# A gated block with a mixture of experts: the last batch's shared network as four steps behind the experts, and integers transposed from the low halves of rounded floats

## What is computed

```python
def smooth_quant_linear(x, w):                    # [T, D] and [O, D] -> [T, O]
    s  = sqrt(max(amax_cols(|x|), EPS) / max(amax_cols(|w|), EPS))
    xs, ws = x / s, w * s
    x_scale = max(amax_rows(|xs|), EPS) / 127     # w_scale likewise
    x_q = clip(round(xs / x_scale), -127, 127)    # w_q likewise
    return x_q @ w_q.T * x_scale * w_scale.T

def layer(x, guw, dw):                            # one batch; guw 512x512, dw 512x256
    gate, up = split(smooth_quant_linear(x, guw))
    return smooth_quant_linear(silu(gate) * up, dw)

def moe(x):                                       # 2048 tokens; 16 experts, top 2, capacity 256
    w, e = top_k(softmax(x @ gate_w.T), 2)
    y  = the two experts' outputs of each token, times w
    sh = (silu(x @ ws_gate) * (x @ ws_up)) @ ws_down         # inner size 704
    return y + sh                                            # an expert's inner size is 352

x = x + tanh(g_xattn) * layer(layernorm(x), fside, ctx)      # per batch
x = x + tanh(g_ffn) * moe(layernorm(x))
```

## Time and profile before

| | before |
|---|---|
| median of three runs | 679.56 us (679.54 to 680.46) |
| the profiled execution | 680.59 us |
| its span, first to last instruction | 678.9 us |
| PE busy | 519.1 us, 76% of the span |
| DVE busy | 423.3 us, 62% |
| ACT busy | 291.3 us, 43% |
| POOL busy | 156.1 us, 23% |
| mean granted clock of TensorE | 0.909 |
| moved by DMA | 83.32 MB, mean 123 GB/s |

### The profile page before, as it was taken

How to read it: one execution, slowest core, us unless ns; L and a number is a source line. 1 busy time by engine, 2 the same in 40 slices (tenths; PEclk the granted TensorE clock), 3 DMA queues, 4 the chain that set the end, 5 groups by cost and what they waited for, 6 DMA issues and landing times.

```text
span 678.9 us, 8404 instructions
## 1 busy us (share of the span) xinstructions
PE 519.1 (76%) x3080; PEld 423.7 (62%) x3080; DVE 423.3 (62%) x633; ACT 291.3 (43%) x402; POOL 156.1 (23%) x138
## 2 busy tenths in 40 slices
PE   0363424799899989899789999999999999994000
PEld 0232322588557866587557889999999999994000
DVE  5667788596677757642658486666666666660354
ACT  2267553426632673243232145566556655651000
POOL 2311454022000400010000151231122113001773
PEclk9995765999899998999899989999999999998555
DMA  7810103001110001300100157776787677602776
GB/s 288 308 62 0 32 0 124 1 1 32 62 63 0 31 0 62 127 1 0 63 0 1 32 175 239 254 242 202 254 262 239 192 263 259 202 31 81 244 246 233
DMA packets 42200, 83.32 MB, mean 123 GB/s; under 512 B 4081, under 2 KB 22513, under 8 KB 41153
## 3 DMA queue, kind: packets, MB, share of 16 engines
q1 hardware_dynamic: 37056, 66.23, 28.4%
q0 software_dynamic: 5120, 16.78, 8.1%
HBM read 66.23 MB, written 16.78 MB: 122 GB/s over the span
## 4 chain that ended last, share of the span: by engine, by line
PE 64%; DVE 15%; ACT 8%; issue 6%; POOL 5%; DMA 1%; POOLq 0%; DVEq 0%
PE ps_gu L1098 12%; PE ps_gu L1100 12%; PE ps_gu L1099 12%; PE ps_d L1098 5%; PE ps_d L1100 5%; PE ps_d L1099 5%; POOL got L484 4%; PE ps_a L1137 2%; PE ps_a L1332 2%; DVE y L745 1%; PE ps_a L1144 1%; DVE bn_b L734 1%; DVE sh_hid L819 1%; PE ps_a L1198 1%; ACT w L517 1%
## 5 line engine op out<-in xcount | busy, mean ns | idle before, releaser
L1098 PE MATMUL ps_gu<-ex_xhi,w_hi 128*128 128x256 f32 (+1 forms) x384 | 110.3, 287 | 1.1 <-DVE ex_xlo L1038 1.1
L1099 PE MATMUL ps_gu<-ex_xlo,w_hi 128*128 128x256 f32 (+1 forms) x384 | 107.9, 281 | 0.0
L1100 PE MATMUL ps_gu<-ex_xhi,w_lo 128*128 128x256 f32 (+1 forms) x384 | 107.7, 281 | 0.0
L1098 PE MATMUL ps_gu<-xt_hi,sw_hi 128*128 128x512 f32 x176 | 72.0, 409 | 7.5 <-DVE sh_hid L819 7.2
L1098 PEld LDWEIGHTS ps_gu<-ex_xhi,w_hi 128*128 128x128 f32 (+1 forms) x384 | 69.6, 181 | 6.1 <-issue 3.9
L1099 PEld LDWEIGHTS ps_gu<-ex_xlo,w_hi 128*128 128x128 f32 (+1 forms) x384 | 69.5, 181 | 0.7
L1100 PEld LDWEIGHTS ps_gu<-ex_xhi,w_lo 128*128 128x128 f32 (+1 forms) x384 | 69.7, 181 | 0.0
L1099 PE MATMUL ps_gu<-xt_lo,sw_hi 128*128 128x512 f32 x176 | 68.9, 392 | 0.0
L1100 PE MATMUL ps_gu<-xt_hi,sw_lo 128*128 128x512 f32 x176 | 68.9, 391 | 0.0
L453 POOL DMA_INDIRECT xg<-x2n_scratch,idx_col x32 | 52.1, 1629 | 18.0 <-POOL idx_col L449 13.1
L1024 DVE TENSOR_TENSOR w_lo<-raw_gu,w_hi 128x1408 fp32r<-128x1408 f32 x32 | 51.6, 1616 | 0.0
(11 more groups left out here) (234 smaller groups left out, 1129.4 us busy)
## 6 DMA issues: line engine op xcount, KB each, us to landing
raw_gu<-in_L_ffn_w_gate SPq DMA_DIRECT2D x16, 704.0 KB
raw_gu<-in_L_ffn_w_up SPq DMA_DIRECT2D x16, 704.0 KB
raw_d<-in_L_ffn_w_down SPq DMA_DIRECT2D x16, 512.0 KB
expert_out_scratch<-eo SPq DMA_DIRECT2D x16, 512.0 KB
w<-in_fside_BxS2xS SPq DMA_DIRECT2D x4, 1024.0 KB, 5.2
x2n_scratch<-y SPq DMA_DIRECT2D x4, 1024.0 KB, 3.9
out<-x SPq DMA_DIRECT2D x8, 512.0 KB
x<-in_x SPq DMA_DIRECT2D x1, 3072.0 KB, 16.8
```

The lines of the kernel that those rows point to most:

```text
L1098: pe.matmul(dst, a_hi, b_hi, start=start, stop=False)
L1099: pe.matmul(dst, a_hi, b_lo, start=False, stop=False)
L1100: return pe.matmul(dst, a_lo, b_hi, start=False, stop=stop)
```

## The change

1. *Rounding.* `rounded` goes. `quantise` adds 16384 with the magic number, so the low 16 bits of each rounded float are 16384 plus the integer. PE transposes these low halves directly as bfloat16 (every second one), and `integers` reads the bank as 16-bit integers and takes 16384 off. The semaphores `x_scaled` and `w_scaled` go, and the loads of `w1` and `w2` wait for the transposes.
2. *Shared network.* The last iteration does only chunks 0 to 2 of batch 2's shared network, the routing's stage chunks 3 to 5 of it. Batch 3's shared network becomes four steps E to E+3 behind the experts, with an expert's sizes: 256 tokens (steps E, E+2 the first half, E+1, E+3 the second) by 352 of the inner size (E, E+1 the first, E+2, E+3 the second). The weights of a half are loaded and split once, its tokens too. DVE adds each step's result from `ps_d` to `x2` (`shared_rows`). Batch 3's transposed tokens for the router go to their own place (`xt3_hi`, `xt3_lo`).
3. *End.* `got` holds three batches. POOL's gathers start when all experts' rows are stored, beside the four steps, and `add_rows` is written out between and behind the steps' DVE work.

The diff, cut to its core:

```diff
+LOW16 = 16384.0
...
+    got = [place(cur, "got0", [P, J, 2, D]), place([region], "got1", [P, J, 2, D]), place([shared], "got2", [P, J, 2, D])]
+    FL, FM = B - 2, 3
+    NE, NW = E + 4, E + 2
...
-            sp.wait_ge(qw_done[LA], 1)
+            sp.wait_ge(full[LA], unit(LA, 0, A_QW + 1))
             load_w1(1)
...
-            sp.wait_ge(sh_gu, MS * B)
+            sp.wait_ge(sh_gu, MS * (FL + 1))
             load_raw(1, 1)
...
+            def load_tokens(e, q):
+                sp.wait_ge(ex_xt, e - 1)
+                j = slice((e - E) * HALF, (e - E + 1) * HALF)
+                sp.dma_start(xg[q][:], x2n_v[B - 1][:, j, :]).then_inc(xf_in[q], 16)
...
+            store_eo(E - 4, 0)
+            split_done(E - 2)
+            load_shared(E, 0)
+            load_tokens(E, 0)
+            store_eo(E - 3, 1)
+            split_done(E - 1)
+            load_shared(E + 1, 1)
+            load_tokens(E + 1, 1)
+            store_eo(E - 2, 0)
+            store_eo(E - 1, 1)
...
             gather_rows(0, 0)
+            pool.wait_ge(ex_wlo, 2 * E + 2)
+            pool.wait_ge(ex_wdlo, E + 1)
             gather_rows(1, 1)
-            with pool.Fori(1, B // 2) as r:
-                for k in range(2):
-                    pool.wait_ge(summed, 2 * (2 * r + k - 1))
-                    gather_rows(2 * r + k, k)
+            pool.wait_ge(ex_wlo, 2 * NW)
+            pool.wait_ge(ex_wdlo, NW)
+            pool.wait_ge(got_in[0][0], 16 * J)
+            pool.wait_ge(got_in[0][1], 16 * J)
+            gather_rows(2, 2)
+            pool.wait_ge(got_in[1][0], 16 * J)
+            pool.wait_ge(got_in[1][1], 16 * J)
+            pool.wait_ge(summed, 2)
+            gather_rows(3, 0)
...
                 for j in range(J):
-                    last = act.activation(src[:, j, :], src[:, j, :], ACT.Copy, bias=MAGIC, scale=inv[:, j:j + 1])
-                last.then_inc(scaled, 1)
-                rounded(b, src, dst, scaled, done)
+                    last = act.activation(src[:, j, :], src[:, j, :], ACT.Copy, bias=MAGIC + LOW16, scale=inv[:, j:j + 1])
+                last.then_inc(done, 1)
...
-                src = bank(layer, n0 + u, wide).bitcast(BF16)
+                src = bank(layer, n0 + u, wide).bitcast(I16)
                 act.activation(dst[:, 2 * u:2 * u + 2, :], src.rearrange("p (c t) -> p c t", c=2),
-                               ACT.Copy).then_inc(free[layer], 1)
+                               ACT.Copy, bias=-LOW16).then_inc(free[layer], 1)
...
-            iteration(None, B - 1, B - 2)
+            iteration(None, B - 1, FL, FM)
...
+            def shared_rows(e):
+                dve.wait_ge(ex_d, M * e + M)
+                if e >= E + 2:
+                    dve.wait_ge(ex_eo, e - 1)
+                for h in range(HALF):
+                    j = e % 2 * HALF + h
+                    last = dve.scalar_tensor_tensor(out=x2[:, B - 1, j, :], in0=ps_d[:, 2 * (e % 2) + h, :], scalar=tg[:, 1:2],
+                                                    in1=x2[:, B - 1, j, :], op0=ALU.mult, op1=ALU.add)
+                last.then_inc(ex_eo, 1)
...
+            hidden(E + 2, 0, 0)
+            shared_rows(E + 1)
+            hidden(E + 2, 0, 1)
+            add_rows(0, 0)
+            hidden(E + 2, 0, 2)
+            add_rows(0, 1)
+            hidden(E + 3, 1, 0)
+            shared_rows(E + 2)
+            hidden(E + 3, 1, 1)
+            add_rows(1, 0)
+            hidden(E + 3, 1, 2)
+            add_rows(1, 1)
+            add_rows(2, 0)
+            add_rows(2, 1)
+            shared_rows(E + 3)
+            dve.wait_ge(ex_eo, NE)
+            add_rows(3, 0)
+            add_rows(3, 1)
...
-                        last = pe.transpose(out16[:, at:at + P], src[:, j, c * P:(c + 1) * P], ident_b[:])
+                        last = pe.transpose(out16[:, at:at + P], src[:, j, c * P:(c + 1) * P].bitcast(BF16)[:, 0:2 * P:2], ident_b[:])
...
-            sh_up(f, 0)
-            sh_up(f, 1)
-            sh_down(f, 0)
+            sh_up(f, FM)
             pe.wait_ge(seq_done, 1)
...
-            sh_up(f, 2)
-            sh_down(f, 1)
+            sh_up(f, FM + 1)
+            sh_down(f, FM)
...
             table(0, NPOS)
-            sh_up(f, 3)
-            sh_down(f, 2)
             table(NPOS, 2 * NT)
-            sh_up(f, 4)
-            sh_down(f, 3)
-            sh_up(f, 5)
-            sh_down(f, 4)
+            sh_up(f, FM + 2)
+            sh_down(f, FM + 1)
...
+            for e in range(E, NE):
+                q, w = e % 2, weights_of(e)
+                up(e, q, 0, w=w)
+                down(e - 1, 1 - q, 2, w=weights_of(e - 1))
+                up(e, q, 1, w=w)
+                down(e, q, 0, w=w)
+                if e == E:
+                    turn_tokens(e + 1, E // 2, 1)
+                up(e, q, 2, w=w)
+                down(e, q, 1, w=w)
+            down(NE - 1, 1, 2, w=NW - 1)
```

More of the change, by code:

```diff
@@ L578, in sh, with iteration @@
                 act.activation(sh_hhi[0:k, m % RING, :], sh_hid[0:k, m % 2, :], ACT.Copy).then_inc(sh_hi, 1)
-            def iteration(a, b, f):
+            def iteration(a, b, f, chunks=MS):
                 def sh_chunk(m):
-                    if f is not None:
+                    if f is not None and m < chunks:
                         sh(f, m)
@@ L697, in _ @@
                 step(2 * r + 2, r + 1, 0)
-            step(E - 1, E // 2 - 1, 1, last=True)
+            step(E - 1, E // 2 - 1, 1)
+            weights_gu(E + 1, E // 2, 1)
+            hidden(E, 0, 0, False)
             rows_out(E - 1, E // 2 - 1, 1)
+            hidden(E, 0, 1, False)
+            tokens(E + 1, 1)
+            hidden(E, 0, 2, False)
+            weights_d(E + 1, 1)
+            for e in range(E + 1, NE):
+                for m in range(M):
+                    hidden(e, e % 2, m, False)
         @block.vector
@@ L914, in iteration @@
                     dve.tensor_tensor(gated[:], gated[:], xn[:, :, I2:D], ALU.mult).then_inc(gated_done, 1)
-                if f is not None:
+                if f is not None and chunks == MS:
                     sh_add(f)
@@ L1070, in _, with add_rows @@
                 step(2 * r + 2, 0)
-            step(E - 1, 1, last=True)
-            def add_rows(b, r, k, half):
-                dve.wait_ge(got_in[k][half], 16 * J * (r + 1))
+            step(E - 1, 1)
+            def shared_rows(e):
[7 more added lines that the diff above has]
+                last.then_inc(ex_eo, 1)
+            def add_rows(b, half):
+                k = b % 3
+                dve.wait_ge(got_in[k][half], 16 * J * (b // 3 + 1))
                 x2_b, w_b = x2[:, b], wts[:].rearrange("p n (b j) -> p b n j", j=J)[:, b]
@@ L1083, in add_rows @@
                 for j in tiles:
-                    last = dve.scalar_tensor_tensor(out=x2_b[:, j, :], in0=got[:, k, j, 1, :], scalar=w_b[:, 1, j:j + 1],
+                    last = dve.scalar_tensor_tensor(out=x2_b[:, j, :], in0=got[k][:, j, 1, :], scalar=w_b[:, 1, j:j + 1],
                                                     in1=x2_b[:, j, :], op0=ALU.mult, op1=ALU.add)
                 last.then_inc(summed, 1)
-            with dve.Fori(0, B // 2) as r:
-                for k in range(2):
-                    for half in range(2):
-                        add_rows(2 * r + k, r, k, half)
+            hidden(E, 0, 0)
+            weights_gu(E + 1, 1, 0)
+            hidden(E, 0, 1)
+            tokens(E + 1, 1)
+            weights_gu(E + 1, 1, 1)
+            hidden(E, 0, 2)
+            weights_d(E + 1, 1)
+            for m in range(M):
+                hidden(E + 1, 1, m)
+                if m == 0:
+                    shared_rows(E)
+            hidden(E + 2, 0, 0)
[16 more added lines that the diff above has]
+            add_rows(3, 1)
         @block.tensor
@@ L1174, in sh_down, with iteration @@
                     last.then_inc(sh_ring, 1)
-            def iteration(a, b, f):
+            def iteration(a, b, f, chunks=MS):
                 def up(*chunk):
-                    if f is not None:
+                    if f is not None and chunk[0] < chunks:
                         sh_up(f, *chunk)
                 def down(*chunk):
-                    if f is not None:
+                    if f is not None and chunk[0] < chunks:
                         sh_down(f, *chunk)
@@ L1268, in iteration @@
                         pe.wait_ge(router_lo, 1)
+                    hi, lo = (xt_hi, xt_lo) if a is not None else (xt3_hi, xt3_lo)
                     for c in range(C):
-                        last = three(bank(LB)[0:E, :], gate_hi[:, c, :], gate_lo[:, c, :], xt_hi[:, c, :], xt_lo[:, c, :],
+                        last = three(bank(LB)[0:E, :], gate_hi[:, c, :], gate_lo[:, c, :], hi[:, c, :], lo[:, c, :],
                                      c == 0, c == C - 1)
```

150 lines of the change are left out of this document (79 added, 71 removed).

## The result

In its timed group the changed kernel took 684.76 us (median of 7 runs, 682.16 to 685.98), the kernel before 679.54 (678.51 to 680.46): 1.0069 times as long, with an interval of 1.0049 to 1.0088, so 0.7% slower where 1.6% faster was forecast. The profiled execution took 682.49 us with a span of 680.8.

The account below looks back on a forecast made before the run. PE was taken to bound all phases up to the end, with DVE's chain close behind in routing, and GpSimd the gather tail. Terms 0 - 7.1 - 15.3 + 11.7 = -10.7 us gave 668.9 us, 1.6% faster; range 660 to 677.

Parts of the forecast that it names:

- part 5: The end: four new steps beside the gathers, PE ending at T+53, DVE's list bounding the end at T+72.5; +11.7 us.
- T: Start of the first of the four new shared-network steps behind the experts; 618.2 us in the profile before.
- rival A: Gathers bound the end: GpSimd's issues, slowed beside busy DVE, add 14 us, giving 683 us, slower; chance 0.10.
- Part 1: Rounding: second ScalarE passes go in all four batches, 7.1 us gained; strided transposes counted at no extra cost.
- rival B: Strided transpose loads cost what float32 ones do, +11.9 us: 681; half that price 675. Chance 0.12, half for each.
- Parts 2 and 3: Last iteration and routing, each losing three shared-network chunks of PE work: 15.3 us gained, the rest lost to DVE's chain.
- cold terms: Last iteration and routing: PE's clock drops after idling, slowing token transposes, logits and rank matmuls; about 5 us.
- rival C: PE stays warm, or the routing's chain is shorter: 664 us; chance 0.12.
- rival D: Removed cover shows nothing because an unseen wait holds the experts' start: about 679 us, no change; chance 0.06.
- Part 4: The sixteen experts: unchanged, 13.5 us a step with PE full.

Follow-up runs that it names:

- group E: The changed kernel unedited, 670.71 us (ratio 0.9865), beside the same with 256 PE instructions added, 670.57 us (0.9866), on one chip; neither stalled.
- e1: The kernel before with the rounding change alone, shared network left in place: 674.19 us, ratio 0.9903.
- group F: The changed kernel with the first three batches' additions of gathered rows each one step earlier: 668.14 us, ratio 0.9807 to the kernel before.
- group B: On another chip, changed kernel unedited 682.34 us; four additions behind hidden chunks 693.23; third gather held until third new step done 681.79; additions one step later 688.84.
- groups A, C and D: Changed kernel with additions moved, gathers held, broken up or replaced by plain loads, or PE instructions added; also rounding alone on the kernel before: 668.54 to 707.47 us.

## Why the prediction was wrong, and where it was right

**The step that failed** is in part 5: "12.6 for the three without a token transpose, so PE ends at T+53". In the result's trace the third step took 25.8 us and PE ended at T+66.8; "End: T+72.5" became T+83.6. Where nothing stalled (group E) PE ended at T+53.4 and the whole at T+70.8. PE ended 13.8 us later than forecast; the rest of the end, 16.8 us where 19.5 were counted behind PE, gave 2.7 back. I took PE's work beside GpSimd's gathers at its price without them. The experts' phase seemed to license that, but there only two gathers are issued per step of 13.5 us; here 24 follow each other. The trace of before has 32 in a row, with PE idle beside them, so it could not show what they do to PE. None of the four rivals held this, and the range ended at 677. That 684.76 lies near the 683 of rival A is chance: A had GpSimd's issues slow, and in the result's trace they take 1.07 us on the mean (1.03 before).

**Part 1.** 7.1 us forecast, 6.6 measured alone. The strided transposes at nothing: 0.62 us per eight, as with dense ones, so rival B is out. The Trainium skill ("TensorE: Matmul & The Clock Gate", section on weight-path perf modes) counts strided non-FP32 columns among those that load fast; the trace agrees: a load takes 98 ns (median) before and after. By terms, from the second layers' first transposes (151.52, 228.05 and 302.88 us before; 148.65, 223.30 and 296.43 in e1): batches 0 and 1 gave 2.9 us (3.6 forecast), batch 2 1.9 and batch 3 1.7 (1.75 each). A second wait of 1.06 us, which I had not counted, is in that.

**Parts 2 and 3.** 15.3 forecast. The first expert started at 379.69, 22.05 us earlier than the earlier trace rows's 401.7; less the 6.6 of part 1 that is 15.5. Each mark was met within 0.4 us: first reduction 332.90 (340.2 less 7.1 was forecast), pos_oh 351.90 (351.9), the end of idx 363.27 (363.5), first expert 379.69 (379.3). The terms written for the first of them add up only to 338.6 of the 340.2. The cold terms, which rival C doubted, were right: token transposes at 1.11 us, after an idle of 9.4 us (9 forecast), and a clock of 0.83 and 0.80 over the two phases. The first expert's start also rules out rival D, which had it held.

**Part 4.** 217.5 us for sixteen steps, 1.0 more than the 216.5 of the earlier trace rows.

**Part 5 where PE isn't stalled.** Gathers start at T+9.5 (9.4), PE ends at T+53.4, the last hidden chunk at T+51.7 (52.3), the last issue at T+59.3 (61). DVE's list bounds the end, as forecast: T+70.8 for 72.5, since one `add_rows` takes 2.8 us where 3.1 were counted. The last gather's rows come 0.49 us late, where 1.3 us in hand were forecast. Span 667.9 for 668.2; 670.7 us for 668.9, inside the range of 660 to 677. That the sum came so close is partly luck: parts 1 to 3 gave 0.35 us less than counted, the experts cost 1.0 more, the end 1.7 less.

**Rival A,** GpSimd slowed by DVE, decides nothing: the 32 issues of the unstalled trace take 1.17 us on the mean, for 1.67 in the rival. But it is there in small: in that trace the last eight take 0.95 to 1.85 us beside additions, and in group F such issues delay the rows that DVE waits for. The tail of before had seven issues of 1.22 to 1.47 us, not the four of 1.3 to 1.4 that the prediction read. The Trainium skill ("SBUF — State Buffer", section "SBUF: two separate sides") says such operations lock each other out, each for a whole instruction. The trace shows issues slowed to 1.3 times on the mean of those eight while DVE works almost without a gap; a lock shows at most as this delay.

**The chances** had a slip of their own: "faster 0.84" counts rival B at its full price, which is 681 us and no change. By the split given there it is 0.78 faster and 0.12 the same.

**What stays open** is what on a chip makes PE's issue and signals late while gathers run. Shown is: the second half of it takes a gather in flight (group B); it belongs to the chip or to what runs beside it (identical programs: 681.5 and 693.2; 670.7 and 682.3); where it is, it is in every execution and at the same group of products; and it lets go about when the gathers' traffic dips. A supply of instructions that is late would look like this, since the new steps are code that is run once. The Trainium skill ("Runtime: NRT & Kernel Launch", section "Instruction fetch mechanics") says that each engine fetches 16 KiB blocks of 256 instructions by its own DMA queue, mostly hidden. An estimate from it, with a weight load to each product, is one block in about 128 products; a step has about 99 products, so that some boundary is near any place. The trace agrees on the size:

```profile
q8 instruction: 15, 0.25, 0.1%
```

That is 16 KB per packet. The packet ahead of the stall was moved in 0.9 us at 618.1, 11 us before PE slowed. But it lies between the last signal on time (617.6) and the first late one (621.7), and so does the start of the second batch's gathers (620.8): the traces don't tell the two apart. The unstalled traces have the packet at the same place of the step. Neither this nor any other cause was shown; the moved code never ran on a stalling chip.

## What to carry to other kernels

A trace in which two things never overlap has no price for their overlap: say so, and give a chance to the outcome in which it costs. When one engine seems to stall, look first at when its signals are taken: here they were late 7 us before its own work was. When a kernel gives two answers, run the same unedited program beside each variant on the same chip before reading anything from the variants; the variants of groups A, C and D each told a clean story and had no common base. Where engine work must overlap a long row of gathers, keep DVE's list short behind the last product (moving four additions behind it cost 10.9 us in group B), and don't queue a wait for gathered rows ahead of what feeds PE (2.86 us in group F).

## What the runs showed of the hardware

- Beside indirect gathers of 256 KB issued one behind the other (10.8 us per eight), PE can be held up in mid-group: gaps of 1.1 to 1.4 us between products, and signals to ScalarE that arrive 1.2, 7.6 and 10.4 us late. The same program on another chip shows nothing. It costs 11.6 to 14 us of 670. Sixteen gathers in a row are enough for the first half of it (the third gather held).
- A kernel without that overlap takes the same time in all these groups (medians 679.5 to 681.0), so its steadiness says nothing of another's.
- Transposes that load every second 16-bit element cost what dense ones do (0.62 us per eight); a copy of 1024 columns of 16-bit integers from PSUM takes 1.02 us, as one of bfloat16 did.
